# Chunks of 128 tokens at both ends of a selective scan that is spread over 59 instead of 57 units

## What is computed

```python
x = x + 0.5 * ffn(layernorm(x))      # W (1024x1024), top 4 of 64 experts of rank 16 (A, B)
x = x + scan_layer(layernorm(x))
x = x + 0.5 * ffn(layernorm(x))      # the same weights again

# scan_layer, per batch, 1024 channels, 16 states each
xz = x @ W_xproj.T                   # 128 ranks, 16 B, 16 C
delta = softplus(xz[:, :128] @ W_dt.T + b_dt)
dA, Bu = exp(delta * A), delta * B * x
h = dA_t * h + Bu_t                  # over the 2048 tokens in order
y = sum(h * C_t) + x * D
```

## Time and profile before

| what | before |
|---|---|
| median of 3 runs | 2759.53 us (2757.13 to 2759.86) |
| the profiled execution | 2758.88 us, of it 2757.1 us span |
| TensorE, matrix products | 2586.1 us busy (94%) |
| GpSimd | 2349.9 us busy (85%) |
| VectorE | 2219.7 us busy (81%) |
| ScalarE | 1501.3 us busy (54%) |
| granted clock of TensorE | 0.993 over the span |

### The profile page before, as it was taken

The page is one execution under the profiler, slowest core; times in us unless marked ns, Lnnn a source line. Parts: engine busy times, 40 slices in busy tenths (PEclk is TensorE's granted clock), DMA queues, the critical chain, the costliest instruction groups (busy, mean ns, idle before and its releaser), DMA issues.

```text
span 2757.1 us, 39894 instructions
## 1 busy us (share of the span) xinstructions
PE 2586.1 (94%) x13593; PEld 1170.8 (42%) x13664; DVE 2219.7 (81%) x2933; ACT 1501.3 (54%) x3363; POOL 2349.9 (85%) x703
## 2 busy tenths in 40 slices
PE   4989999999999999999999999999999999899999
PEld 1444444444434444444444444444444444444444
DVE  7448888888888888888888888888888888888943
ACT  5346667665555655655556555565555555556511
POOL 1138999899989999999999999999999999999910
PEclk9999999999999999999999999999999999999999
DMA  5144544644464545554454445544455445454321
GB/s 217 55 116 152 151 137 141 179 146 139 143 166 143 154 127 155 154 150 143 144 169 137 143 143 170 155 149 133 146 170 151 157 128 156 141 146 153 92 62 54
DMA packets 333217, 390.29 MB, mean 142 GB/s; under 512 B 149459, under 2 KB 249939, under 8 KB 333014
## 3 DMA queue, kind: packets, MB, share of 16 engines
q1 hardware_dynamic: 316118, 354.18, 43.0%
q10 hardware_dynamic: 16896, 33.56, 4.1%
HBM read 250.82 MB, written 103.29 MB: 128 GB/s over the span
## 4 chain that ended last, share of the span: by engine, by line
PE 36%; DVE 34%; ACT 8%; DVEq 7%; issue 7%; DMA 4%; POOL 2%; ACTq 1%; SPq 0%; POOLq 0%
DVE mreg L1154 18%; PE pv L560 12%; PE po L560 7%; PE pv L564 6%; PE po L564 4%; ACT pA L940 3%; PE py L727 3%; DMA delta_scratch<-mreg 2%; DVE pv L1114 2%; DVE sel L1111 2%; DVEq L1119 2%; DVEq L1069 2%; DVE ln_st L1068 1%; DVEq L1113 1%; PE pv L689 1%
## 5 line engine op out<-in xcount | busy, mean ns | idle before, releaser
L528 POOL TENSOR_TENSOR mreg<-mreg 128x2048 f32<-128x2048 f32 x256 | 1161.8, 4538 | 96.8 <-ACT hst L926 92.5
L1154 DVE TENSOR_TENSOR_SCAN mreg<-pA,hst,mreg 128x512 f32<-128x512 f32 (+1 forms) x1024 | 1044.2, 1066 | 76.6 <-ACT pA L940 59.0
L940 ACT ACTIVATE pA<-mreg,nA 128x512 f32<-128x512 f32 (+1 forms) x1280 | 739.7, 597 | 398.3 <-DVE mreg L1154 372.0
L518 POOL TENSOR_TENSOR mreg<-mreg 128x1024 f32<-128x1024 f32 x340 | 794.9, 2362 | 122.3 <-DMA mreg<-delta_scratch 109.7
L560 PE MATMUL pv<-wA,xT 128*128 128x512 f16 x2016 | 458.1, 379 | 28.0 <-DVE xT L1091 26.5
L560 PE MATMUL po<-wW,xT 128*128 128x512 f16 x2016 | 469.6, 380 | 4.0 <-issue 0.5
L560 PE MATMUL po<-wB,uT 128*128 128x512 f16 x2016 | 465.8, 379 | 7.9 <-DVE xin L1077 7.4
L512 POOL TENSOR_TENSOR mreg<-mreg 128x2048 f32<-128x2048 f32 x86 | 389.5, 4529 | 5.5 <-issue 5.2
L560 PEld LDWEIGHTS pv<-wA,xT 128*128 128x128 f16 x2016 | 190.8, 98 | 305.9 <-ACT xT L847 65.8
L560 PEld LDWEIGHTS po<-wB,uT 128*128 128x128 f16 x2016 | 191.3, 98 | 266.3 <-issue 36.4
L560 PEld LDWEIGHTS po<-wW,xT 128*128 128x128 f16 x2016 | 196.0, 98 | 240.1 <-issue 26.3
(11 more groups left out here) (132 smaller groups left out, 2371.7 us busy)
## 6 DMA issues: line engine op xcount, KB each, us to landing
mreg<-delta_scratch SPq DMA_DIRECT2D x256, 512.0 KB, 5.2
mreg<-xnT_scratch SPq DMA_DIRECT2D x128, 256.0 KB, 4.9
delta_scratch<-mreg ACTq DMA_DIRECT2D x128, 256.0 KB
xin<-x SPq DMA_DIRECT2D x32, 512.0 KB, 4.2
x_scratch<-xin SPq DMA_DIRECT2D x32, 512.0 KB, 3.0
xnT_scratch<-auxs SPq DMA_DIRECT2D x32, 512.0 KB, 2.9
yT_scratch<-mreg SPq DMA_DIRECT2D x64, 256.0 KB, 5.6
uT<-yT_scratch SPq DMA_DIRECT2D x32, 512.0 KB, 5.2
```

Source lines behind the costliest of these rows:

```text
L518: pool.tensor_tensor(h[:, half * n:half * n + n, :], u, b.broadcast_to([P, n, c.width]), ALU.mult).then_inc(s_bm, 1)
L528: pool.tensor_tensor(h, h, by_c, ALU.mult).then_inc(s_cm, 1)
L940: last = nc.scalar.activation(dst[:, part, :], src[:, part, :], ACT.Exp, scale=nA[:, m:m + 1])
L1154: last = V.tensor_tensor_scan(h, split(pA[:, i % 2, :], c)[:, part, :], h, before, ALU.mult, ALU.add)
```

## The change

Chunks of one row are added: the first two and last two chunks of the scan hold 128 tokens, with tiles of four parts of 128 tokens (8 of the 64 tiles). Only the two neighbours of these at each end, one chunk at each, keep 256 tokens (8 tiles instead of 16); the 48 tiles of 512 tokens stay. The scan begins in unit 2 and ends with unit 60. Units 2 to 9 have 16 blocks each, one tile, and units 10 to 60 share the other 896 blocks, 17 or 18 each, 17.57 in the mean. Two deltas in a unit now fall in units 3, 5, 9, 14, 24, 34, 44 and 54, and units 4 and 8 have none. An assertion on how late a delta may be made is dropped, and `scan` waits for the states kept 8 groups before instead of 16.

```diff
-SCAN0 = 3
-SCAN1 = 60
-SIZES = ((2, 2, 4, 4, 4), (4, 4, 4, 2, 2))
+SCAN0 = 2
+SCAN1 = 61
+RAMP = 8
+SIZES = ((1, 1, 2, 4, 4, 4), (4, 4, 4, 2, 1, 1))
...
-    slot_unit, first = {}, 0
+    starts = [16 * n for n in range(RAMP)]
+    rest = SCAN1 - SCAN0 - RAMP
+    starts += [16 * RAMP + n * (4 * NGRP - 16 * RAMP) // rest for n in range(rest + 1)]
+    slot_unit = {}
     for u in range(SCAN0, SCAN1):
-        last = (u + 1 - SCAN0) * NGRP // (SCAN1 - SCAN0)
-        for n in range(first, last):
-            slot_unit[n] = (u, n - first)
-        first = last
+        groups = [n for n in range(NGRP) if starts[u - SCAN0] <= 4 * n < starts[u + 1 - SCAN0]]
+        for i, n in enumerate(groups):
+            slot_unit[n] = (u, i)
...
-        a.block0 = (a.u - SCAN0) * 4 * NGRP // (SCAN1 - SCAN0)
-        a.block1 = (a.u + 1 - SCAN0) * 4 * NGRP // (SCAN1 - SCAN0)
+        a.block0, a.block1 = starts[a.u - SCAN0], starts[a.u + 1 - SCAN0]
...
-        elif t > 2:
-            u, i = slot_unit[4 * t - 6]
-            assert at <= ((u, 0) if i == 0 else (u, 1) if i < 3 else (u + 1, 0)), (t, at)
...
                 if s == 0:
                     dve.wait_ge(s_bm, 2 * G + 2)
-                    dve.wait_ge(s_sv, max(G - 15, 0))
+                    dve.wait_ge(s_sv, max(G - 7, 0))
```

## The result

The changed kernel takes 2780.38 us (median of 4 runs, 2777.38 to 2783.90), the kernel before 2759.70 in the same comparison: 1.0076 times as long, 95% interval 1.0058 to 1.0093, or 20.7 us more. The profiled execution took 2778.48 us, of it 2776.7 us span. The forecast was 2776.

The account below looks back on a forecast made before the run. No single engine was taken as the bound: TensorE and VectorE share the chain, with a loop through ScalarE. Terms -35.7, +44.9, -17.3, +58.7 and -33.9 sum to +16.7 us, giving 2776 us, range 2745 to 2800.

Parts of the forecast that it names:

- The start: Up to the first unit with a scan: unit without scan work or wait for tile 0 drops out, -35.7 us.
- The price of an instruction more: Narrow tiles: each extra scan, decay and their like costs 0.133 us at the tail, 0.09 where TensorE sets a floor.
- The first eight units: Units 2 to 9: narrower tiles, fewer blocks, 358.3 us where units 3 to 9 took 313.4, +44.9 us.
- The middle: Units 10 to 52: 0.35 us less in each of 43 units, one fewer with two deltas, -17.3 us.
- The tail: Units 53 to 60: narrower tiles and one unit more, 362.8 us against 304.1 before, +58.7 us.
- the 46.5 to 48 that I had named as the sign: Units 57 to 60: mask-to-mask time of 46.5 to 48 us would confirm the forecast.
- The end: After the scan: one unit without a scan less, -33.9 us.
- TensorE's issue: Narrow groups' sums on TensorE: pairs can't issue below 0.067 us, 2793 us in all; chance 0.10.
- the estimate of 2.6 us: Narrow group's sum on TensorE, by the skill's 81 ns a pair at 128 columns.
- Late deltas: Tiles 1, 2, 4, 8: deltas made just ahead of their scan, four boundaries with up to 8 us, 2802 us; chance 0.08.
- The shadow case: Extra instructions stay in VectorE's and TensorE's shadow; eight narrow units fall about 2 us each, 2760 us; chance 0.14.
- GpSimd as the leader of the middle: Units 10 to 52: GpSimd leads, fewer blocks save 38 us instead of 15, 2745 us in all; chance 0.22.

Follow-up runs that it names:

- the run with the chunk sizes alone: Kernel before with only the change's chunk sizes and the matching wait for kept states, scan still in units 3 to 59: 2795.28 us, 1.0126.
- The head alone: Kernel before with two chunks of one row at the start and scan from unit 2, its old tail kept: 2766.79 us, 1.0023.
- the tail alone: Kernel before with two chunks of one row at the end and scan to unit 60, its old head kept: 2783.05 us, 1.0083.
- the last two runs: Changed kernel with second delta's magnitudes behind the high part and `AHEAD = 9`: 2757.52 us; the same with scan ending at unit 59: 2760.64 us.
- `AHEAD = 11`: Kernel before with deltas made from 11 groups ahead instead of 10: 2790.95 us, 1.0114.
- the changed kernel with the moved magnitudes: Changed kernel with the second delta's magnitudes on ScalarE behind the two copies of the next unit's high part: 2762.44 us, 1.0006.

## Why the prediction was right, and where it wasn't

The sign, the size and the main reason held: 16.7 us were forecast and 19.7 came in the profiled execution, 20.7 in the medians, because narrow tiles cost more instructions at both ends than two more units for the scan give back. That the total came within 3 us is partly luck: two terms were off by 10 and 18 us, against each other. By its steps:

- *The start*, moved by one unit: -35.7 against -36.7. Of this 1.9 us lie ahead of unit 0's mask (61.67 against 63.58) and have nothing to do with the change.
- *The price of an instruction more*, 0.133 us, was right in the mean: the run with the chunk sizes alone gives 0.136. At the tail this mean is made of one dear unit and of others at 0.08 us. The fixed parts carried on from 512 and 256 columns were right: a scan of 128 columns has 0.389 us of busy time and a decay 0.307, where 0.39 and 0.31 were forecast. The groups of L939, L1153 (the fresh chunk's are apart) and L726 at 128 columns, after:

```profile
L939 ACT ACTIVATE pA<-mreg,nA 128x128 f32<-128x128 f32 x512 | 157.2, 354 | 62.7 <-DVE mreg L1153 47.7 <-DMA mreg<-delta_scratch 9.7 <-issue 5.2
L1153 DVE TENSOR_TENSOR_SCAN mreg<-pA,hst,mreg 128x128 f32<-128x128 f32 x384 | 149.5, 461 | 6.4 <-ACT pA L939 6.2
...
L726 PE MATMUL py<-mreg,Em 128*32 128x128 f32 x1024 | 35.4, 280 | 1.1 <-DVE mreg L1164 1.1
```

- *The first eight units* were 10 us too dear. The term that was mis-sized is what two blocks fewer are worth: I took 1.2 us of 1.2 to 2.5, and a TensorE floor of 42.4 us. Units 6 to 8 took 40.4, 41.6 and 40.2 us, unit 8 with TensorE busy all the time, where 42.4, 42.4 and 41.3 were forecast. That units on the loop gain from all scans and not from half fits this, but no run varied their blocks alone.
- *The middle* is the step that failed: -17.3 against +0.8. What I left out is that a unit with two deltas has no fixed price: I took 2.3 to 3.2 us from before, and it was 5.4 in the middle, since the second delta's magnitudes wait longer for the first one's write. I had read SyncE's wait for that write, but not ScalarE's for the same one, 5.5 us over the span. The other part of the term, 0.35 us a unit for 0.39 blocks less, had the size right (0.29 in units with one delta) and probably the reason wrong. The head alone keeps 17.92 blocks and has 0.24 of these 0.29; the tail alone has 17.66 and nothing of them; the later end, 0.35 blocks less, brings 0.04 in the last two runs. So the gain comes with the head of the change. `AHEAD`, which moves the deltas, leaves it as it is. What in the head brings it stays open.
- *The tail*: +58.7 against +53.9, two errors again. The narrow units 57 to 60 took 44.8, 46.1, 44.4 and 45.0 us, some 2 us less each than the terms of the sum and below the 46.5 to 48 that I had named as the sign. Unit 54, with two deltas, took 47.5 where the sum had 43.7: it had no term for them.
- *The end*: -33.9 against -33.1.

The rivals. TensorE's issue falls: a narrow group's sum is 32 pairs of 0.035 us, 1.11 us, against 1.07. The 81 ns of the Trainium skill ("TensorE: Matmul & The Clock Gate", Back-to-back issue gap), and with them the estimate of 2.6 us, don't hold for these weights of 32 columns in four column groups; the measurement decides. Late deltas fall too: ScalarE's decays wait 11.2 us for a delta's read, 9.7 of them at the start, where 15.8 were waited before. GpSimd waited for it more often, 15 times instead of 8, and yet the first eight units came out below the forecast. The shadow case, some 2 us for each of eight narrow units, falls with the 34.7 us of the chunk sizes alone. GpSimd as the leader of the middle falls: its wait for kept states grew, in units 10 to 52 from 57.9 to 87.4 us and over the span from 92.5 us to

```profile
POOL mreg L527 <- ACT hst L925: 147.6, 79, 5.9
```

What stays open: that the reads slow the write is read from two timelines and from what the alignment does; no run moved the reads alone, and the loads of B and C moved with them: from the first of the reads shown to the release there are six after and four before. Why the tail alone is dearer than its account is seen in late transposes, not tested. And a unit with two deltas of 128-token tiles takes 47.2 to 51.5 us in the five runs that have one at the tail; the changed kernel has none there, by the luck of its alignment.

## What to carry to other kernels

When a change shifts the work of one loop against the units of another, look first for the waits whose partner is a DMA, on every engine, and ask what falls next to it after the shift: here one number that moves no work was worth 15 us in one kernel and 30 in the other. A wait for a buffer's write belongs behind what others wait for in the same stream. And a forecast by stages is worth checking by stages: this one hit its total with two errors of 10 and 18 us against each other. The same holds for a stage: the middle's units with one delta came near the forecast for a reason that the runs with other numbers of blocks do not bear out.

## What the runs showed of the hardware

A wait of TensorE may cost its clock too. In the changed kernel's unit 29 TensorE waits 2.3 us for the normalised row, then runs 8 matrix products in 3.32 us instead of 1.89. The timeline and the window with its granted clock:

```profile
1324.80 0.66 PE L551 MATMUL pv<-idf,xn 128*128 128x128 f32 x4 [2.32 <-ACT xn L841]
...
1325.72 3.32 PE L563 MATMUL po<-wB,uT 128*128 128x512 f16 x8
```

```profile
1325.72:1328.97 3.25, 3.25 (x10) 0.96 (x7) 3.09 (x4) 2.45 (x5) 3.25 (x3) 0.55 0.40 107
```

0.55 of full speed is mostly the lower of its two levels, 1.2 GHz. A wait of 2.55 us in the kernel before, at 994 us, left the clock at 1.00, so such a wait doesn't always do it. Over the span the granted clock varies from execution to execution, 0.987 to 0.994 in the kernel before, so only means say something: 0.990 before, 0.988 after, 0.986 with `AHEAD = 11` and 0.991 in the changed kernel with the moved magnitudes, where TensorE's wait for the low part is 26.5, 30.7, 44.9 and 11.1 us. The clock tends to be lower where these waits are longer, which would add to their price; no run tests that by itself.
